# Modulation rows, modulation columns and gates as units of the first iteration, and the QKV weight differences in two parts

## The reference

```python
mod = (_silu(L0_c) @ L0_wmod).reshape(L0_c.shape[0], 6, 1, -1)
sa, ca, ga, sb, cb, gb = (mod[:, 0], mod[:, 1], mod[:, 2], mod[:, 3], mod[:, 4], mod[:, 5])
ga = (2 * (ga >= 0) - 1) * jnp.maximum(jnp.abs(ga), 0.25)
gb = (2 * (gb >= 0) - 1) * jnp.maximum(jnp.abs(gb), 0.25)
h = _layernorm(x, axis=-1) * (1 + ca) + sa
x = x + ga * _L0_attn_ref(h, ...)
h = _layernorm(x, axis=-1) * (1 + cb) + sb
x = x + gb * _L0_ffn_ref(h, L0_ffn_W_fc, L0_ffn_W_proj)
```

## Time and profile before

| | us |
|---|---|
| median of 3 runs | 890.96 (890.9 to 891.18) |
| profiled execution | 887.45 |
| its span, first to last instruction | 885.4 |
| PE busy / weight loads | 820.1 (93%) / 622.8 |
| DVE busy | 586.1 (66%) |
| ACT busy | 612.7 (69%) |
| POOL busy | 206.5 (23%) |

### The profile page before, as it was taken

One profiled execution on the slowest core, in us unless ns is written; L12 is line 12 of the kernel. 1 busy time (PEld: TensorE's weight loads), 2 busy tenths in 40 slices (PEclk: granted clock), 3 DMA queues, 4 the chain that ended last, 5 costly groups with the idle time before them and its releaser, 6 DMA issues.

```text
span 885.4 us, 23955 instructions
## 1 busy us (share of the span) xinstructions
PE 820.1 (93%) x9170; PEld 622.8 (70%) x9170; DVE 586.1 (66%) x1740; ACT 612.7 (69%) x1738; POOL 206.5 (23%) x267
## 2 busy tenths in 40 slices
PE   4786889999999999999999999999999999999976
PEld 1464667678776777778776777677776777767766
DVE  6586763786568756786567756786567766453565
ACT  2355676788667886788667876787767886688633
POOL 3103021220241224120331224120222223200343
PEclk9798999999999999999999999999999999999998
DMA  9400030200022001310022000320022000210110
GB/s 317 148 31 26 4 100 13 91 26 2 26 75 82 25 14 39 102 54 2 26 67 91 25 14 25 97 67 8 21 71 91 25 14 25 61 49 1 37 31 24
DMA packets 32847, 45.35 MB, mean 51 GB/s; under 512 B 3304, under 2 KB 28144, under 8 KB 32512
## 3 DMA queue, kind: packets, MB, share of 16 engines
q1 hardware_dynamic: 29616, 37.53, 12.9%
q0 software_dynamic: 2304, 6.29, 2.3%
q10 hardware_dynamic: 816, 0.00, 0.0%
HBM read 32.52 MB, written 14.97 MB: 54 GB/s over the span
## 4 chain that ended last, share of the span: by engine, by line
PE 76%; DVE 6%; ACT 3%; issue 2%; POOL 1%; DVEq 0%; POOLq 0%; ACTq 0%
PE ps_unit L1059 30%; PE ps_y L1190 10%; PE ps_turned L1243 7%; PE ps_unit L1113 5%; PE ps_scores L1217 4%; PE ps_turned L1265 4%; PE ps_turned L1280 4%; PE ps_unit L1118 3%; PE ps_scores L1226 3%; DVE hn L1474 1%; PE ps_turned L1270 1%; DVE spikes L1491 1%; PE ps_unit L1123 1%; PE ps_unit L1152 1%; DVE loT L1516 1%
## 5 line engine op out<-in xcount | busy, mean ns | idle before, releaser
L990 ACT ACTIVATE probs<-ps_scores,row_min 128x192 f32<-128x192 f32 (+2 forms) x384 | 161.1, 425 | 101.5 <-DVE row_min L1499 54.0
L1000 ACT ACTIVATE probs<-probs,row_inv 128x192 f32<-128x192 f32 (+2 forms) x384 | 155.6, 456 | 0.4 <-DVE row_inv L1509 0.4
L1059 PE MATMUL ps_unit<-xT,wqkv 128*128 128x512 f32 x384 | 109.3, 422 | 2.7 <-POOL xT L798 1.7
L1499 DVE TENSOR_REDUCE row_min<-ps_scores 128x2 f32<-128x512 f32 (+1 forms) x128 | 78.6, 614 | 49.9 <-PE ps_scores L1226 24.3
L1243 PEld LDWEIGHTS ps_turned<-ident,probs 64*128 64x128 f32 x1280 | 56.0, 139 | 75.2 <-issue 65.6
L1190 PE MATMUL ps_y<-wprojT,hid_parts 128*128 128x256 f32 x768 | 104.2, 284 | 1.4 <-POOL hid_parts L563 0.9
L1190 PEld LDWEIGHTS ps_y<-wprojT,hid_parts 128*128 128x128 f32 x768 | 96.5, 188 | 10.0 <-issue 5.8
L1243 PE MATMUL ps_turned<-ident,probs 64*128 64x64 f32 x1280 | 81.5, 238 | 21.5 <-DVE loT L1516 19.1
L1059 PEld LDWEIGHTS ps_unit<-xT,wqkv 128*128 128x128 f32 x384 | 70.8, 194 | 29.5 <-issue 15.5
L1059 PE MATMUL ps_unit<-h_parts,wfcT 128*128 128x512 f32 x336 | 90.1, 403 | 0.1
L1008 ACT ACTIVATE probsT<-ps_turned 128x384 f32<-128x384 f32 x128 | 61.9, 484 | 21.9 <-PE ps_turned L1270 21.9
(11 more groups left out here) (175 smaller groups left out, 1588.2 us busy)
## 6 DMA issues: line engine op xcount, KB each, us to landing
xa<-in_L_attn_x SPq DMA_DIRECT2D x8, 512.0 KB, 4.2
normed_rows<-hn SPq DMA_DIRECT2D x8, 512.0 KB, 3.0
lx<-in_L_attn_x SPq DMA_DIRECT2D x8, 512.0 KB, 3.9
out_x<-spikes SPq DMA_DIRECT2D x16, 256.0 KB, 2.2
hn<-routed_out SPq DMA_DIRECT2D x7, 512.0 KB, 4.1
routed_out<-zero_rows SPq DMA_DIRECT2D x14, 256.0 KB, 4.2
full<-mod_rows SPq DMA_DIRECT2D x7, 256.0 KB, 4.3
gate_a<-mod_rows SPq DMA_DIRECT2D x8, 128.0 KB
```

The lines of the kernel that those rows point to most:

```text
L990: ins = act.activation(probs[:, probs_buffer(n), probs_columns(s, part)], ps_scores[:, part, lo:hi], ACT.Exp, bias=row_min[:, n % 3, part: ...
L1000: ins = act.activation(rows, rows, ACT.Identity, scale=row_inv[:, n % 3, part:part + 1])
L1059: ins = pe.matmul(ps, w(wi, k, w_cols), a(ai, k, a_cols), start=(n == 0), stop=(n == 3 * KD - 1))
L1499: ins = dve.tensor_reduce(row_min[:, n % 3, :], ps_scores[:, :, lo:hi], AX.X, ALU.min)
```

## The change

1. **PE.** MR 1, MR 2 and MC leave `start` and become the first units of slot 0 of the first iteration, after `scores(2)` and ahead of 0NV 2. The wait for the rest of `wmod` goes with them; the wait for `wo_light` and `wo_heavy` goes to LO 0.
2. **DVE.** `weights_low` makes queries and keys first (1024 columns of both halves, counted in `low_made`), and the values (512 columns of both, `values_low`) after z's parts. MR 0 is drained ahead of `second_norm`. The gates become a row stage of slot 1, ahead of `0router1`, and write to other buffers (`spikes`, `hid`, `lx` in place of `v` and `probsT`), so the early value drains no longer wait for the store of the modulation. `low0` moves from slot 0 to slot 2.
3. **SP.** The rest of `wmod` is queued behind `wkv_h`'s half and the zeroes. The modulation's two halves are stored apart: `mod_norm` after `norms_made`, `mod_gate` after `mod_ready`. `raw_wq` is loaded after MR 2 and MC are drained, now within the first iteration; the second half of `w_fc` and one of `w_proj` after the gates' store. `raw_wkv[0]` waits for `values_low` too.
4. **Tables.** HV 1 moves from slot 13 to slot 10; POOL's `pick1` from 21 to 20 and `early0` from 6 to 5. ACT's `routed_weights` stay in slots 1 and 2.

```diff
 FIRST_UNITS = {
-    0: [("0NV", 2)],
+    0: [("MR", 1), ("MR", 2), ("MC", 0), ("0NV", 2)],
...
-    10: [("HK", 0)],
+    10: [("HK", 0), ("HV", 1)],
...
-    13: [("HV", 1), ("RK", 0), ("SR", 1), ("WP", 3)],
+    13: [("RK", 0), ("SR", 1), ("WP", 3)],
...
 FIRST_ROWS = {
-    0: ["low0", "0router0"],
-    1: ["0router1", "0compare0a"],
-    2: ["stats1a", "0compare0b", "stats1b"],
+    0: ["0router0"],
+    1: ["gates", "0router1", "0compare0a"],
+    2: ["low0", "stats1a", "0compare0b", "stats1b"],
...
+            def modulations():
+
+                sp.wait_ge(norms_made, 1)
+                sp.dma_start(mod_rows[:, 0:2 * D], mod_norm).then_inc(mod_stored, 16)
+                store_rows(0)
+                wait_drained(sp, "first", 0, ("MR", 2), ("MC", 0))
+                sp.dma_start(raw_wq, wq_h.rearrange("(k p) n -> p k n", p=P)).then_inc(wr_loaded, 16)
+                sp.wait_ge(mod_stored, 16)
...
                 if first:
-                    store_rows(0)
+                    sp.wait_ge(mod_ready, 1)
+                    sp.dma_start(mod_rows[:, 2 * D:4 * D], mod_gate).then_inc(mod_stored, 16)
+                    sp.wait_ge(mod_stored, 32)
+                    load_wfc(1)
+                    sp.dma_start(raw_wproj[1], w_proj[P:2 * P, :]).then_inc(wproj_loaded, 16)
...
+            def gate_rows(segment, b):
+
+                wait_drained(dve, segment, b, ("MR", 1), ("MR", 2))
+                link(dve.scalar_tensor_tensor(out=gates_abs, in0=gates, scalar=-1.0, in1=gates,
+                                              op0=ALU.mult, op1=ALU.max))
+                link(dve.tensor_scalar(gates_abs, gates_abs, 0.25, None, ALU.max))
+                dve.wait_ge(low_made, KD)
+                dve.wait_ge(values_low, KD)
+                link(dve.tensor_scalar(gates_sign, gates, 0.0, 2.0, ALU.is_ge, ALU.mult))
+                link(dve.scalar_tensor_tensor(out=mod_gate, in0=gates_sign, scalar=-1.0, in1=gates_abs,
+                                              op0=ALU.add, op1=ALU.mult))
+                dve.tensor_scalar(mod_gate[:, D:2 * D], mod_gate[:, D:2 * D], 1.0 / STEPS, None,
+                                  ALU.mult).then_inc(mod_ready, 1)
...
-            weights_low(0)
-            second_norm(0)
             ps, free = drain("start", -1, ("MR", 0))
...
+            second_norm(0)
+            for k in range(KD):
+                weights_low(k, slice(0, 2 * INNER), low_made)
             high_part("start", -1, ("ZT", 0))
             high_part("start", -1, ("ZT", 1))
...
+            for k in range(KD):
+                weights_low(k, slice(2 * INNER, 3 * INNER), values_low)
```

More of the change, by code:

```diff
@@ L186 @@
 }
-FIRST_POOL_SLOTS = {"rstd1": 6, "gather": 5, "rstd2": 14, "norm_rows": 15, "pick0": 15, "pick1": 21, "early0": 6, "early1": 8}
+FIRST_POOL_SLOTS = {"rstd1": 6, "gather": 5, "rstd2": 14, "norm_rows": 15, "pick0": 15, "pick1": 20, "early0": 5, "early1": 8, "high0": 1, "high1": 2}
 FIRST_WEIGHTS = [u for units in FIRST_UNITS.values() for u in units if u[0] in ("WF", "WP")]
@@ L209 @@
     "setup": [("SC", 0), ("MB", 0)],
-    "start": [("MR", 0), ("MR", 1), ("MR", 2), ("ZT", 0), ("ZT", 1), ("MC", 0), ("NQ", 0), ("NK", 0)],
+    "start": [("MR", 0), ("ZT", 0), ("ZT", 1), ("NQ", 0), ("NK", 0)],
     "first": iteration_units(True, False),
@@ L415, in adaln_block_kernel @@
         silu_first = h1[:, 0, :].rearrange("p (k n) -> p k n", k=KD)
-        mod_norm, mod_gate, gates, gates_abs = (v[0:B, i, :] for i in range(4))
-        gates_sign = probsT[0:B, :]
+        mod_norm, mod_gate = (lx[0:B, 2 * i:2 * i + 2, :].rearrange("p t d -> p (t d)") for i in range(2))
+        gates, gates_abs = (spikes[0:B, i, :] for i in range(2))
+        gates_sign = hid[0:B, 2, :]
         ps_scores = ctx.enter_context(nc.psum_tensor("ps_scores", [P, 2, 512], F32))
@@ L604, in _, with load_wfc @@
                              probsT[:, :]).then_inc(out_zeroed, 16)
+            load_wmod(slice(2 * D, 6 * D), wmod_rest_loaded)
             sp.dma_start(wo_light[:, :, :], wo_l.rearrange("(t p) n -> p t n", p=P)).then_inc(wo_loaded, 16)
             sp.dma_start(wo_heavy[:, :, :], wo_h.rearrange("(t p) n -> p t n", p=P)).then_inc(wo_loaded, 16)
-            for i in range(2):
+            def load_wfc(i):
                 sp.dma_start(raw_wfc[i],
@@ L666, in iteration @@
                     sp.dma_start(xa[:, :, :], batch(x, b + 1)).then_inc(x_loaded, 16)
+                    if first:
+                        modulations()
                     sp.wait_ge(xT_low, 2 * b + 2)
@@ L1017, in iteration @@
                     n = SLOTS * b + s
-                    if first and s in (1, 2):
-                        routed_weights(s - 1)
+                    if first and s in (FIRST_POOL_SLOTS["high0"], FIRST_POOL_SLOTS["high1"]):
+                        routed_weights(0 if s == FIRST_POOL_SLOTS["high0"] else 1)
                     if not (first and s == 0):
@@ L1070, in unit @@
                     pe.wait_ge(low_made, LOW_PARTS)
+                if segment == "first" and u == ("MR", 1):
+                    pe.wait_ge(wmod_rest_loaded, 32)
+                if segment == "first" and u == ("0NV", 0):
+                    pe.wait_ge(values_low, KD)
+                if segment == "first" and u == ("LO", 0):
+                    pe.wait_ge(wo_loaded, 32)
                 if segment == "first" and kind == "WF":
@@ L1557, in unit @@
                     dve.tensor_copy(picks[:, n % 2, i, :], ps[:, 0:SEL // P]).then_inc(free, 1)
+                elif kind == "MR":
+                    ps, free = drain(segment, b, u)
+                    columns = slice(0, D) if i == 1 else slice(D, 2 * D)
+                    dve.tensor_copy(gates[:, columns], ps[0:B, columns]).then_inc(free, 1)
+                elif kind == "MC":
+                    ps, free = drain(segment, b, u)
+                    cols = ps[:, 0:4 * B].rearrange("p (q b) -> p q b", q=4)
+                    dve.tensor_copy(shift_b[:, :, :], cols[:, 0:KD, :])
+                    dve.tensor_scalar(scale_b[:, :, :], cols[:, KD:2 * KD, :], 1.0, None, ALU.add).then_inc(free, 1)
                 elif kind in ("LO", "LX"):
```

58 lines of the change are left out of this document (18 added, 40 removed).

## The result

The changed kernel takes **896.69 us** (median of 5 runs, 895.36 to 897.94), the kernel before 890.9 us beside it (5 runs, 889.99 to 891.18). The ratio is 1.0074, with a 95% interval from 1.006 to 1.0087: slower by 0.74%, 5.8 us by the medians. A second set of runs of both gave 1.0078 (1.0062 to 1.0095), 7.0 us by the medians. One run of all those in this document, of the kernel with the new start alone, took 2554.69 us, for a reason that stays open; no ratio counts it. The profiled execution took 896.69 us, its span is 894.7 us.

What follows compares the result with a forecast made beforehand. PE bounds the seven later batches, DVE slots 1 to 4 of the first iteration. +3.1 at 0NV 0, +3.3 gates, +1.5 low0, -1.0 HV 1 make +6.9 us on the profiled 887.45; carried to the median, 897.9 us, range 889 to 903.

Steps and rivals of the forecast that it cites:

- the sum: Whole kernel: +3.1 us at 0NV 0, +3.3 for the gates, +1.5 for low0, -1.0 for HV 1, giving +6.9.
- Start: Up to the first scores: second_norm at 19.2 us, first projection at 25.3 (3.5 earlier), first scores 2.7 us earlier.
- The modulation in slot 0: PE ahead of 0NV 2: MR 1 3.4, MR 2 1.8, MC 2.0, together 7.2 us; MC ends at 43.5.
- `wq_h` behind MC: Slot 1, ACT then PE: raw_wq's load waits for MC's drain, lands at 47.5; 0NV 0 at 50.9, 3.1 us later.
- Gates: Slot 1, DVE behind 0NV 0's drain: no longer covered by PE's projections, paid in full, +3.3 us.
- `low0`: Slot 2, DVE: 1.8 us moved from slot 0, 0.3 of it in idle time, +1.5 us.
- HV 1: PE, slot 13 to slot 10: its 1.67 us product fits PE's 2.05 us wait in slot 10, -1.0 us.
- Slots 3 to 24: After low0 (+7.9 us in all) only HV 1 changes the lateness (-1.0); pick1, early0 and moved loads cost nothing.
- The clock: Rival: PE's half-rate stretches vanish through long products in its idle beginning, together -9.8 us, 888.1; chance 0.13.
- DVE's additions: Rival: PE and ACT set the pace through slot 4, gates and low0 fall into DVE's waits; 892 to 893; chance 0.15.
- The worse case: Rival: half rate through MR 2 and MC (+3 us), back in slot 2 (+1.3 per projection); 902; chance 0.15.
- the rule of shared ports: Start: by the page DVE's first difference could wait for POOL, under 1.5 us; the prediction took nothing for it.

Runs made afterwards that it cites:

- the kernel with the new start alone: Kernel before with only the start's new order; MR 1, MR 2, MC, gates, low0 and raw_wq's load stay where they were: 887.53 us, ratio 0.9986.
- the kernel with fillers in three waits: Kernel before with the start's new order and HV 1 in slot 10, plus nine PE products in three waits: 885.34 us, ratio 0.9959.

## Why the prediction was right, and where it was not

The forecast was 897.9 us, the measurement 896.69; the sum said +6.9 us on the path, the two comparisons 5.8 and 7.0 us. By its steps:

1. *Start.* `second_norm` 19.18 (forecast 19.2), first projection 25.11 (25.3), the products of queries and keys 4.86 us (5.1). MR 1 at 36.25 (36.3). Right.
2. *The modulation in slot 0.* 3.25 + 1.8 + 1.8 = 6.9 us (7.2), 0NV 2 at 43.12 (43.5), and MR 1 in fact at the lower level, MR 2 at the higher. Right.
3. *`wq_h` behind MC.* ACT begins at 47.47 (47.5), 0NV 0 at 50.81 (50.9). Right, and shown by moving it: the chain costs 1.5 us at 0NV 0. The prediction gave it 0.8, since it had PE alone later than it was.
4. *Gates.* Forecast +3.3, measured +2.5. The term was mis-sized: the steps are shorter in their new place. The four on 8x512 take 0.67, 0.41, 0.42 and 0.68 us here; in the kernel before they take 0.67, 0.60, 0.58 and 0.84, and nearly the same in the kernel with the new start alone (0.72, 0.59, 0.58, 0.84). In both of those POOL works on `hn` beside them, and they write to `v` and `probsT` instead of `spikes`, `hid` and `lx`. No run separates the two, so that POOL is the reason is not shown.
5. *`low0`.* Forecast +1.5, measured +1.2: its 1.73 us fill all of the 0.5 us that DVE was idle in slot 2 and not 0.3 of them. With the gates' 0.8 and this 0.3 slot 3 comes 6.65 us late and not 8 (7.9 by the sum).
6. *HV 1.* Forecast -1.0. In the rows of the changed kernel it is there (7.8 us late at slot 13, 6.7 at slot 14), in the time it isn't: putting it back changed nothing, and moving it alone changed nothing. The failed step is that it took PE's 1.67 us as pure cost in slot 13 and as free in slot 10, both at the full clock. Without them slots 13 and 14 took 7.4 to 7.8 instead of 6.9 to 7.1 us at a lower granted clock in six of eight profiles, and in slot 10 they took 2.0 to 2.6 us where the clock was low.
7. *Slots 3 to 24.* The prediction carried the sum through them unchanged. In the profiles it grew by 1.3 us between slots 8 and 11 and by 1.7 us in slot 18, both at a lower granted clock (0.64 in the window of 95 us; 0.61 in slot 18, where the kernel before has 1.00 in one profile and 0.58 in the other). That makes the two profiled executions 9.3 us apart where the medians are 5.8. The second profile of the changed kernel shows that this growth belongs to the execution. The head of its slot 19:

```profile
134.81 0.16 DVE L1528 RECIPROCAL row_inv<-row_sum 128x2 f32<-128x2 f32 x1
```

Against the kernel before (first profile) it is 7.2 us late at slot 3 and 7.1 us at slots 8, 11, 13, 18 and 19, and its span is 7.5 us longer. So the sum was in fact carried through nearly unchanged there, though HV 1's gain is missing in it: slots 13 and 14 together take 7.4 us.

That the forecast came within 1.2 us of the measurement is in part luck: terms 4 and 5 were 1.1 us too large, and the 1.0 us of term 6 did not come.

*The rivals.* The clock did not pay back: it was 0.85, 0.66 and 0.64 in the windows above, no better than before. DVE's additions were not covered where the change puts them; ahead of 0NV 0's copy they are. The worse case, half rate through MR 2 and MC, did not come: MR 2 took 1.8 us.

On the rule of shared ports that the prediction weighed, POOL's timeline of the changed kernel speaks:

```profile
18.06 1.01 POOL L748 TENSOR_TENSOR rstd<-veps,neg_half 128x4 f32<-128x4 f32 x1
...
20.37 3.91 POOL L767 TENSOR_TENSOR rstd<-veps,neg_half 128x4 f32<-128x4 f32 x1
```

The second operation began 0.1 us ahead of DVE's first weight difference, and lasted until 24.28 us, through both differences and the three steps behind them. In the kernel with the new start alone DVE's differences begin only at 21.14 us, and the same operation took 1.09 us:

```profile
20.35 1.09 POOL L755 TENSOR_TENSOR rstd<-veps,neg_half 128x4 f32<-128x4 f32 x1
```

It takes 3.91 us in all six profiles of the changed kernel and its variants and 1.08 to 1.09 us in the eight others. DVE lost nothing: its differences took 1.22 us each, as in the earlier trace rows. So here DVE kept going and POOL, which by the trace began first, was held up. The Trainium skill, page "SBUF — State Buffer", section "Who interferes with whom", says that the one that issues first has the ports and the other blocks. By the order of the starts in this trace DVE would have waited, and it did not; but the starts are only 0.1 us apart, and the order of issue isn't in the trace. The prediction's reading, nothing for DVE, was right. For the time it is nothing, as POOL's next step waits for DVE's xT anyway.

## What to carry to other kernels

Before a step is moved out of a start-up stretch, read what it waits for there: three units that cost 0.6 us among the waits of the start cost 6.9 us in a slot where PE sets the pace, and their buffer held back a load that ACT and then PE waited for. Small steps go ahead of a wait for another engine, not behind it: the same gates and weights cost 3.7 us behind a copy and nothing ahead of it. And a product taken out of a stretch where PE waits anyway may cost in clock what it saves in work; look at the granted clock of the slots behind before the saving is counted.

## What the runs showed of the hardware

- **Short waits of PE and its clock.** With waits of 0.31 to 0.60 us in slot 12 and 0.83 us in slot 13, the granted clock of slot 13 was 0.55 to 0.64 in six of eight profiles, and slots 13 and 14 took 7.4 to 7.8 us; in the two others, with the same waits, it stayed at 1.00 and they took 6.0. With three more products in the second wait it stayed at 1.00 in both profiles. Two profiles are few against two of eight; the time of the kernel with fillers in three waits, 2 us less, is the stronger sign.
- **It is not fixed by the program.** The same twelve products took 4.27 and 5.46 us in two executions of the kernel before, and slot 18 5.3 and 7.3 us. In fourteen profiles slot 18 fell six times (6.5 to 7.7 us) and eight times not (5.2 to 5.3 us). One profile can't show a gain of 1 us here.
- **DVE against POOL.** A POOL operation on 128x4 took 3.91 instead of 1.09 us beside DVE's operations with two inputs, although it began first by the trace.
